# Gate of five experts as seven block products, on one Trainium2 core

## The chip, the cores and the metric

One core of a Trainium2 chip runs one program that computes a whole block: adaptive layer norm, attention, a second adaptive layer norm and a mixture of eight experts. The metric is the time of one execution in device microseconds. Lower is better.

## The reference, cut to what matters

All arrays are float32. x is 8 x 256 x 256 (batch, sequence, width), so 2048 tokens of width 256. The last part is this, with T = tokens, D = 256, E = 8 experts, F = 256, R = 64 and NL = 2 experts with low-rank terms:

```python
weights = _router_weights(x, Wr, temperature)
gate = jnp.einsum('btd,edf->ebtf', x, Wg)
up = jnp.einsum('btd,edf->ebtf', x, Wu)
gate = gate.at[:NL].add(jnp.einsum('btd,edr,erf->ebtf', x, Ga, Gb))
up = up.at[:NL].add(jnp.einsum('btd,edr,erf->ebtf', x, Ua, Ub))
mid = jax.nn.silu(gate) * up
out = jnp.einsum('ebtf,efd->ebtd', mid, Wd)
out = out.at[:NL].add(jnp.einsum('ebtf,efr,erd->ebtd', mid[:NL], Da, Db))
return jnp.einsum('bte,ebtd->btd', weights, out)
```

## The kernel before

Matrix products are made of three: an operand is split into a rounded part ("hi", type FP32R) and the remainder ("lo"), and `three` (lines 537 to 542) issues hi x hi, hi x lo and lo x hi into one place in PSUM. Each matmul has a weight load of 128 x 128.

Attention runs over 64 slots (batch b, pair of heads), slots 0 to 65 with the pipeline's ends. From slot 59 on, the first expert tiles are woven in. A tile is one expert and 512 tokens (n = 0 to 3); there are 32, in the order of `TILES`: experts 0 and 1 for n = 0 to 2, then (0, 3) and (1, 3), then experts 2 to 7 with four tiles each. In the kernel's numbering (`ORDER`) the experts with low-rank terms are 2 and 3. Tiles 0 to 3 lie in the slots; from tile 4 (`NEXT`) on a loop of its own runs on each engine (TensorE L839, ScalarE L1132, VectorE L1546, GpSimd L1724). FIRST_OF[2] is tile 8 and FIRST_OF[7] is tile 28.

In each tile m TensorE issues `up(2m)` and `up(2m+1)` (for each half of F, gate then up, 12 matmuls of 512 columns in all for each half), then `down(2m-2)` and `down(2m-1)` of the tile before (12 matmuls of 256 columns each). `ps_s` holds gate and up of one half, `ps_proj` those of the other. ScalarE makes the silu of the gate from PSUM (`gate_of`), VectorE multiplies with up (`product`), ScalarE rounds the result (`mid_head`), VectorE makes the remainder (`mid_tail`), and after the down matmuls VectorE adds the weighted result to `acc` (`accumulate`). For tiles 4 to 7 the router of the last tokens lies between these on VectorE (`LATE_ROUTE`) and ScalarE.

The weights of an expert are loaded to `raw_e`, two buffers that alternate by expert; `split_e` rounds a third of them on ScalarE and makes the remainder on GpSimd (L1660). These splits stand at the tiles of `EXPERT_STEPS`, all three of an expert at one tile, two tiles ahead of its first. The low-rank factors (64 rows) are multiplied in FP32 by `low_rank` (L756 to L766), two matmuls of 256 columns for each of six products (each is recorded as two instructions), and VectorE's `fold` adds the result to `raw_e` ahead of the split. `h2_tail` of the last batch is VectorE's remainder of the normalised tokens; tile 6 waits for it.

Every engine works through its own list in order, and all order between engines is by semaphores written out by hand. Near the end GpSimd works out the rest of the output (`rest_of_output`, `last_part`), which uses `part` of expert 7.

## Time and profile before

| | us |
|---|---|
| median of 3 runs | 808.46 |
| lowest, highest | 808.2, 809.51 |
| the profiled execution | 808.01 |
| its span | 806.3 |
| busy: TensorE | 795.3 |
| busy: VectorE | 507.5 |
| busy: ScalarE | 462.2 |
| busy: GpSimd | 395.0 |

The span is the time from the first to the last recorded instruction. In the profile PE is TensorE, PEld its weight loads, DVE VectorE, ACT ScalarE, POOL GpSimd, SP SyncE. Matmuls overlap their neighbours: what one costs is the distance between two starts, not its length.

### The profile page before, as it was taken

What the parts mean: (1) busy time and instruction counts of PE and PEld (TensorE: products, weight loads), DVE (VectorE), ACT (ScalarE), POOL (GpSimd) and SP (SyncE); (2) the same over time, 40 slices, a digit from 0 to 9 for tenths busy, and PEclk for the clock granted to TensorE, in tenths of its full rate; (3) what the DMA queues carried; (4) which work ended last, traced back from release to release, by engine and by line L of the source; (5) the groups of instructions that cost most, each with busy time, mean ns of one, the idle gap of its engine ahead of it and who ended that gap; (6) DMA issues with size and microseconds to landing.
All of it is one profiled execution on the core that took longest, in us unless ns stands there. A gap on an engine that the chain in (4) does not pass through costs nothing.

```text
span 806.3 us, 14755 instructions
## 1 busy us (share of the span) xinstructions
PE 795.3 (99%) x5116; PEld 710.1 (88%) x5116; DVE 507.5 (63%) x1074; ACT 462.2 (57%) x1255; POOL 395.0 (49%) x543
## 2 busy tenths in 40 slices
PE   9899999999999999999999999999999999999997
PEld 8688898999999999999999999899888888888887
DVE  5677676476476566557557658667785454454575
ACT  5777686677577677667767776643343232332322
POOL 3777587486576667567567656120011010110493
PEclk9999999999999999999999999999999999999999
DMA  9200010000000000000000000203010110100002
GB/s 333 103 28 2 1 61 1 1 8 2 0 8 2 1 7 2 2 2 6 1 1 8 1 2 2 79 1 94 38 40 2 40 40 1 40 0 1 1 1 105
DMA packets 8170, 21.53 MB, mean 27 GB/s; under 512 B 1561, under 2 KB 4249, under 8 KB 7969
## 3 DMA queue, kind: packets, MB, share of 16 engines
q1 hardware_dynamic: 7520, 20.51, 7.5%
q8 instruction: 42, 0.69, 0.4%
q14 instruction: 32, 0.25, 0.1%
q10 hardware_dynamic: 576, 0.08, 0.1%
HBM read 18.48 MB, written 2.11 MB: 26 GB/s over the span
## 4 chain that ended last, share of the span: by engine, by line
PE 93%; DVE 2%; POOL 1%; ACT 1%; issue 1%; DMA 1%; ACTq 0%; DVEq 0%; POOLq 0%
PE ps_o L663 14%; PE ps_proj L540 9%; PE ps_proj L542 9%; PE ps_proj L541 9%; PE ps_s L540 7%; PE ps_s L541 7%; PE ps_s L542 7%; PE ps_turn L592 4%; PE ps_y L540 4%; PE ps_y L541 4%; PE ps_y L542 4%; PE ps_turn L610 3%; PE ps_turn L540 2%; PE ps_turn L541 2%; PE ps_turn L542 2%; PE ps_o L542 2%
## 5 line engine op out<-in xcount | busy, mean ns | idle before, releaser
L663 PE MATMUL ps_o<-vaug,probs 128*128 128x129 f32 x1024 | 135.3, 275 | 1.6 <-POOL probs L1654 0.9
L663 PEld LDWEIGHTS ps_o<-vaug,probs 128*128 128x128 f32 x1024 | 129.1, 191 | 8.0 <-POOL probs L1654 1.4
L984 ACT ACTIVATE ps_s<-ps_s,knorm 128x512 f32<-128x512 f32 x128 | 79.1, 657 | 95.7 <-PE ps_s L542 95.5
L1267 DVE RECIPROCAL rden<-ps_o 128x2 f32<-128x2 f32 x128 | 21.8, 170 | 154.0 <-PE ps_o L663 153.9
L1660 POOL TENSOR_TENSOR we_lo<-raw_e,we_hi 128x512 fp32r<-128x512 f32 x22 | 28.4, 1316 | 182.3 <-ACT we_hi L1027 182.3
L1237 DVE TENSOR_TENSOR prod<-ps_proj,cs 128x1024 f32<-128x1024 f32 x76 | 92.5, 1217 | 10.9 <-ACT sq L927 10.9
L1605 POOL TENSOR_TENSOR root<-ssq,powers 128x4 f32<-128x4 f32 x76 | 77.7, 1023 | 27.6 <-ACT sq L927 27.6
L927 ACT ACTIVATE sq<-ps_proj 128x128 f32<-128x128 f32 x304 | 79.9, 278 | 18.2 <-PE ps_proj L542 15.2
L1621 POOL TENSOR_TENSOR prod<-prod 128x512 f32<-128x512 f32 x62 | 80.0, 1290 | 9.9 <-DVE prod L1237 9.9
L540 PE MATMUL ps_proj<-w_hi,h_hi 128*128 128x512 f32 x192 | 83.1, 433 | 0.9 <-DVE w_lo L1180 0.5
L1652 POOL TENSOR_SCALAR_AFFINE_SELECT probs<-probs 128x256 f32<-128x256 f32 x64 | 26.3, 410 | 106.1 <-ACT probs L992 105.8
L540 PE MATMUL ps_y<-wo_hi,oT_hi 128*128 128x256 f32 x256 | 75.8, 296 | 0.0
L542 PE MATMUL ps_proj<-w_hi,h_lo 128*128 128x512 f32 x192 | 75.7, 394 | 0.0
L541 PE MATMUL ps_proj<-w_lo,h_hi 128*128 128x512 f32 x192 | 75.4, 393 | 0.0
L1628 POOL TENSOR_TENSOR rows<-prod,rnorm 128x512 f32<-128x512 f32 x62 | 66.7, 1075 | 13.2 <-issue 4.7
L542 PE MATMUL ps_y<-wo_hi,oT_lo 128*128 128x256 f32 x256 | 71.4, 279 | 0.0
L541 PE MATMUL ps_y<-wo_lo,oT_hi 128*128 128x256 f32 x256 | 71.4, 279 | 0.0
L1044 ACT ACTIVATE mid_hi<-mid 128x512 fp32r<-128x512 f32 x64 | 40.2, 629 | 47.9 <-DVE mid L1352 26.0
L992 ACT ACTIVATE probs<-ps_s 128x1024 f32<-128x1024 f32 x64 | 66.2, 1035 | 0.0
L927 ACT ACTIVATION_READ_ACCUMULATOR sq<-ps_proj 128x1 f32 x304 | 63.4, 209 | 0.0
L1271 DVE TENSOR_TENSOR o_rows<-ps_o,rden 128x256 f32<-128x256 f32 x128 | 54.3, 424 | 4.4
L540 PE MATMUL ps_proj<-h_hi,we_hi 128*128 128x512 f32 x140 | 55.6, 397 | 0.0
(212 smaller groups left out, 2178.1 us busy)
## 6 DMA issues: line engine op xcount, KB each, us to landing
raw_e<-in_we SPq DMA_DIRECT2D x8, 768.0 KB, 4.3
raw_p<-in_wqkv SPq DMA_DIRECT2D x6, 512.0 KB, 8.1
raw_e<-in_wo SPq DMA_DIRECT2D x4, 512.0 KB, 11.6
x_all<-in_x SPq DMA_DIRECT2D x1, 1536.0 KB, 7.0
out<-acc SPq DMA_DIRECT2D x3, 512.0 KB, 2.6
x_all<-in_wmod SPq DMA_DIRECT2D x1, 1024.0 KB, 10.0
gates_a<-gate_rows_dram SPq DMA_DIRECT2D x8, 128.0 KB, 2.9
gates_b<-gate_rows_dram SPq DMA_DIRECT2D x1, 1024.0 KB, 8.0
```

The costliest lines, as they stand in the source:

```text
L540: pe.matmul(dst, hi, w_h, start=first, stop=False, skip_group_check=True)
L541: pe.matmul(dst, hi, w_l, start=False, stop=False, skip_group_check=True)
L542: return pe.matmul(dst, lo, w_h, start=False, stop=last, skip_group_check=True)
L663: mm = pe.matmul(ps_o[:, h * (D + 1):(h + 1) * (D + 1)], probs[:, s % 2, at:at + P], vaug[b % 2][:, k, i // 2, :], start=(h == 0 and k == ...
L927: squared = act.activation(sq[:, n % 2, h, :], ps_proj[:, u % 2, h * D:(h + 1) * D], ACT.Square, accum_out=ssq[:, n % 2, h:h + 1])
L984: act.activation(ps_s[:, t, :], ps_s[:, t, :], ACT.Tanh, scale=knorm[:, b % 2, t, i // 2:i // 2 + 1]).then_inc(tanh_done, 1)
L992: act.activation(probs[:, s % 2, :], ps_s[:].rearrange("p k n -> p (k n)"), ACT.Exp, scale=CAP).then_inc(exp_done, 1)
L1237: dve.tensor_tensor(prod[:, n % 2], src, cs[:, t].unsqueeze(2).broadcast_to([P, 2, 4, D]), ALU.mult).then_inc(rotated, 1)
L1271: dve.tensor_tensor(o_rows[:, t], o[:, :, 0:D], rden[:, t, :].unsqueeze(2).broadcast_to([P, 2, D]), ALU.mult).then_inc(o_rows_ready, 1)
L1605: pool.tensor_tensor(root[:, n % 2, :], ssq[:, n % 2, :], powers[:, 0:4], ALU.pow).then_inc(root_ready, 1)
L1621: pool.tensor_tensor(whole, whole, turned, ALU.add).then_inc(rot_sum, 1)
L1628: pool.tensor_tensor(rows[:, n % RING], prod[:, n % 2, 0], rnorm[:, n % 2, :].unsqueeze(2).broadcast_to([P, 4, D]), ALU.mult).then_inc(row ...
```

## The change

For the tiles 8 to 27 (experts 2 to 6) the gate is no longer made of 12 matmuls of 512 columns. The gate's weights (256 x 256) are taken as 2 x 2 blocks A of 128 x 128 and the tokens (256 x 512) as 2 x 2 blocks B of 128 x 256, and the result comes from seven block products, 21 matmuls of 256 columns, of blocks and of sums of blocks (S1 to S4 of A, T1 to T4 of B). Four products come first in the tile (`seven_first`), ScalarE copies them to SBUF (`copy_seven`), GpSimd adds pairs of them (`sums_seven`), then come the up matmuls, one down half, the last three products on top of what is in PSUM (`seven_last`) and the other down half. VectorE adds to two quarters (`add_quarters`); ScalarE makes the silu of one quarter from PSUM and of the other three at once, in place (`silu_seven`). Up always uses `ps_s`, the products `ps_proj`.

The sums need work of their own: `sums_t` (GpSimd, four operations of 128 x 256 for each n, for n = 0 and 1 in slots 63 and 64), `round_t` and `rest_t` (two operations of 128 x 512 each on ScalarE and GpSimd), `sums_s` (GpSimd, four of 128 x 128 for each expert), `round_s` and `rest_s` (128 x 512). The splits of an expert are spread, one side task in each tile. For n = 2 the tokens are written to DRAM from ScalarE's queue in slots 59 and 60 and read back.

The low-rank factors are loaded twice, to partitions 0 to 63 and 64 to 127; in A the lower half holds the rounded part and the upper the remainder, and B is rounded and its remainder made (`low_round`, `low_rest`). One product is then four matmuls of 256 columns in FP32R with 128 rows instead of two in FP32 with 64. They stand at tiles 5 (one), 6 (two), 7 (one) and 8 (two), before at 5 (two), 6, 8 and 9 (two). `part` gets a buffer for each n.

```diff
...
-LOW_STEPS = {NEXT + 1: [0, 1], NEXT + 2: [2], NEXT + 4: [3], NEXT + 5: [4, 5]}
+LOW_STEPS = {NEXT + 1: [0], NEXT + 2: [1, 2], NEXT + 3: [3], NEXT + 4: [4, 5]}
...
+SEVEN, EIGHT = FIRST_OF[NL], FIRST_OF[NE - 1]
+SEVEN_SPLIT = {FIRST_OF[e - 1] + at: (e, m3) for e in range(NL + 1, NE) for m3, at in enumerate((0, 1, 3))}
+SEVEN_SUMS = {FIRST_OF[e - 1] + 1: e for e in range(NL + 1, NE - 1)}
+SEVEN_ROUND = {FIRST_OF[e - 1] + 2: e for e in range(NL + 1, NE - 1)}
...
-                if (was := last_with(up_pair, g)) is not None:
+                if m == EIGHT:
+                    pe.wait_ge(mid_done, 2 * EIGHT)
+                elif (was := last_with(up_pair, g)) is not None:
...
+            def seven_first(m):
+                e, n = TILES[m]
+                q = m - SEVEN
+                of = blocks(m)
+                if m == FIRST_OF[e]:
...
+                    pe.wait_ge(t_split, 2 * n + 2)
+                if q:
+                    pe.wait_ge(quarter_silu, 2 * q - 1)
+                else:
+                    pe.wait_ge(mid_done, 2 * SEVEN)
+                product_of(ps_proj[:, 0, 0:S], of["A11"], of["B11"], True)
+                product_of(ps_proj[:, 0, S:], of["S2"], of["T2"], False).then_inc(seven_ready, 1)
+                if q:
+                    pe.wait_ge(quarters_added, q)
+                product_of(ps_proj[:, 1, 0:S], of["S1"], of["T1"], True)
...
+            def seven_last(m):
+                q = m - SEVEN
...
+                pe.wait_ge(seven_copied, 2 * q + 1)
+                product_of(ps_proj[:, 0, 0:S], of["A12"], of["B21"], False).then_inc(gu_ready, 1)
+                pe.wait_ge(seven_copied, 2 * q + 2)
+                product_of(ps_proj[:, 1, 0:S], of["S4"], of["B22"], False)
+                product_of(ps_proj[:, 1, S:], of["A22"], of["-T4"], False).then_inc(gu_ready, 1)
...
+                for f in range(2):
+                    pe.wait_ge(mid_done, 2 * SEVEN if m == SEVEN else 2 * m - 1 + f)
+                    for k in range(KT):
+                        mm = three(ps_s[:, f, :], we_hi[e % 2][:, 2 + k, f * P:(f + 1) * P], we_lo[e % 2][:, 2 + k, f * P:(f + 1) * P],
...
                 for k in range(KT):
...
+                    pe.matmul(dst, lowA_both[:, e, m3, at], lowB_hi[:, e, m3, :], start=(k == 0), stop=False, skip_group_check=True)
+                    mm = pe.matmul(dst, lowA_both[:, e, m3, at], lowB_lo[:, e, m3, :], start=False, stop=True, skip_group_check=True)
                 mm.then_inc(low_ready, 1)
...
+            for m in range(SEVEN, EIGHT):
+                seven_first(m)
+                up_alone(m)
+                down(2 * m - 2)
+                seven_last(m)
+                down(2 * m - 1)
+                for i in LOW_STEPS.get(m, ()):
+                    low_rank(i)
...
+            def round_t(n):
+                act.wait_ge(t_made, 4 * n + 4)
...
+                for b in range(2):
+                    act.activation(t_hi[n][:, b], h2s[n][b][:], ACT.Copy).then_inc(t_hi_done, 1)
...
+            def copy_seven(m):
+                q = m - SEVEN
...
+                    act.wait_ge(quarters_added, q)
+                for bank in range(2):
+                    act.wait_ge(seven_ready, 2 * q + bank + 1)
+                    act.activation(seven[:, 2 * bank:2 * bank + 2, :].rearrange("p a n -> p (a n)"), ps_proj[:, bank, :], ACT.Copy).then_inc(seven_copied, 1)
+            def silu_seven(m):
...
+                act.wait_ge(gu_ready, 4 * m + 3)
+                act.activation(silu[:, 0, 0:S], ps_proj[:, 0, 0:S], ACT.Silu).then_inc(quarter_silu, 1)
+                act.wait_ge(last_quarter, q + 1)
+                act.wait_ge(quarters_added, q + 1)
+                others = silu[:].rearrange("p f n -> p (f n)")[:, S:]
+                act.activation(others, others, ACT.Silu).then_inc(quarter_silu, 1)
...
+                act.activation(lowA_both[:, e], lowA[:, e], ACT.Copy).then_inc(low_rounded, 1)
+                act.activation(lowB_hi[:, e], lowB[:, e], ACT.Copy).then_inc(low_rounded, 1)
...
-                for e, m3 in EXPERT_STEPS.get(m, ()):
-                    split_e(e, m3)
+                    low_round(0)
+                    round_t(0)
+                if m == NEXT + 1:
+                    low_round(1)
+                if m == NEXT + 2:
+                    split_e(NL, 0)
+                    round_t(1)
+                if m == NEXT + 3:
+                    round_s(NL)
+                    split_e(NL, 1)
+                    split_e(NL, 2)
+                    round_t(2)
+            for m in range(SEVEN, EIGHT):
+                copy_seven(m)
+                if m in SEVEN_SPLIT:
+                    split_e(*SEVEN_SPLIT[m])
+                if m in SEVEN_ROUND:
+                    round_s(SEVEN_ROUND[m])
+                if m == SEVEN + 1:
+                    round_t(3)
+                silu_seven(m)
+                mid_head(2 * m)
...
+            def add_quarters(m):
...
+                dve.wait_ge(gu_ready, 4 * m + 4)
...
+                dve.tensor_tensor(silu[:].rearrange("p f (a n) -> p (f a) n", a=2)[:, 1:3, :], ps_proj[:, 1, :].rearrange("p (a n) -> p a n", a=2),
+                                  seven[:, 0:1, :].broadcast_to([P, 2, S]), ALU.add).then_inc(quarters_added, 1)
+            def product_seven(g):
...
+                dve.tensor_tensor(mid[:, f, :], ps_s[:, f, :], silu[:, f, :], ALU.mult).then_inc(mid_done, 1)
...
-                    dve.wait_ge(final_add, 2 * n + half - 1)
...
+            for m in range(SEVEN, EIGHT):
+                accumulate(2 * m - 2)
+                add_quarters(m)
+                for g in (2 * m, 2 * m + 1):
+                    product_seven(g)
+                for g in (2 * m, 2 * m + 1):
+                    mid_tail(g)
+                accumulate(2 * m - 1)
+                for i in LOW_STEPS.get(m, ()):
+                    fold(i)
...
+            def sums_t(n):
...
+                pool.tensor_tensor(b21, b21, b22, ALU.subtract).then_inc(t_made, 1)
...
+            def low_rest(e):
...
+                pool.tensor_tensor(lowA_both[R:P, e], lowA[R:P, e], lowA_both[R:P, e], ALU.subtract).then_inc(low_split, 1)
...
+                pool.tensor_tensor(lowB_lo[:, e], lowB[:, e], lowB_hi[:, e], ALU.subtract).then_inc(low_split, 1)
...
+            def rest_t(n):
...
+                    pool.wait_ge(t_hi_done, 2 * n + b + 1)
+                    pool.tensor_tensor(t_lo[n][:, b], h2s[n][b][:], t_hi[n][:, b], ALU.subtract).then_inc(t_split, 1)
+            def sums_s(e):
...
+                pool.wait_ge(we_split, 3 * e - 1)
+                pool.tensor_tensor(a22, a21, a22, ALU.add).then_inc(s_made, 1)
...
+                pool.tensor_tensor(a12, a12, a11, ALU.subtract).then_inc(s_made, 1)
+            def rest_s(e):
+                pool.wait_ge(s_hi_done, e - NL + 1)
+                pool.tensor_tensor(s_lo[e % 2][:], raw_e[:, e % 2, 0:KT, :], s_hi[e % 2][:], ALU.subtract).then_inc(s_split, 1)
+            def sums_seven(m):
...
+                pool.wait_ge(seven_copied, 2 * q + 1)
+                pool.tensor_tensor(seven[:, 0, :], seven[:, 0, :], seven[:, 1, :], ALU.add).then_inc(u_made, 1)
+                pool.wait_ge(seven_copied, 2 * q + 2)
+                pool.tensor_tensor(seven[:, 2, :], seven[:, 2, :], seven[:, 3, :], ALU.add).then_inc(pair_made, 1)
...
+                pool.wait_ge(mid_done, 2 * m)
+                pool.tensor_tensor(silu[:, 1, S:], seven[:, 0, :], seven[:, 2, :], ALU.add).then_inc(last_quarter, 1)
...
-            for m in range(NEXT, len(TILES)):
-                for e, m3 in EXPERT_STEPS.get(m, ()):
-                    split_e(e, m3)
+            low_rest(0)
+            rest_t(0)
+            low_rest(1)
+            split_e(NL, 0)
+            sums_s(NL)
+            rest_t(1)
+            sums_t(2)
+            rest_s(NL)
+            split_e(NL, 1)
+            split_e(NL, 2)
+            rest_t(2)
+            for m in range(SEVEN, EIGHT):
+                sums_seven(m)
+                if m in SEVEN_SUMS:
+                    sums_s(SEVEN_SUMS[m])
+                if m in SEVEN_SPLIT:
+                    split_e(*SEVEN_SPLIT[m])
+                if m in SEVEN_ROUND:
+                    rest_s(SEVEN_ROUND[m])
+                if m == SEVEN:
+                    sums_t(3)
+                if m == SEVEN + 2:
+                    rest_t(3)
             for n in range(LATE):
...
```

## Rows read from the trace of the kernel before

**Rows 1.** The profile's page: busy us, share and instructions; granted clock in 40 slices; chain.

```profile
PE 795.3 (99%) x5116; PEld 710.1 (88%) x5116; DVE 507.5 (63%) x1074; ACT 462.2 (57%) x1255; POOL 395.0 (49%) x543
...
PEclk9999999999999999999999999999999999999999
...
PE 93%; DVE 2%; POOL 1%; ACT 1%; issue 1%; DMA 1%; ACTq 0%; DVEq 0%; POOLq 0%
```

**Rows 2.** Stretches: us, busy PE PEld DVE ACT POOL, clock, DMA share, GB/s.

```profile
30.00:40.00 10.00, 7.95 (x45) 5.49 (x44) 5.26 (x10) 7.79 (x25) 9.52 (x14) 1.00 0.52 188
706.57:714.93 8.36, 8.36 (x50) 7.38 (x49) 4.34 (x9) 2.35 (x4) 0.00 (x0) 1.00 0.00 0
740.08:748.52 8.44, 8.44 (x51) 7.34 (x49) 4.31 (x9) 2.35 (x4) 0.00 (x0) 1.00 0.01 2
765.40:773.68 8.28, 8.28 (x50) 7.34 (x49) 5.69 (x9) 2.35 (x4) 8.04 (x7) 1.00 0.01 2
```

**Rows 3.** TensorE in order of time: start, length, line, operation, out<-in.

```profile
593.93 0.39 PE L540 MATMUL ps_s<-h_hi,we_hi 128*128 128x512 f32 x1
...
706.57 0.40 PE L540 MATMUL ps_s<-h_hi,we_hi 128*128 128x512 f32 x1
...
712.06 0.28 PE L540 MATMUL ps_turn<-we_hi,mid_hi 128*128 128x256 f32 x1
...
740.08 0.39 PE L540 MATMUL ps_s<-h_hi,we_hi 128*128 128x512 f32 x1
...
745.67 0.28 PE L540 MATMUL ps_turn<-we_hi,mid_hi 128*128 128x256 f32 x1
...
748.52 0.39 PE L540 MATMUL ps_s<-h_hi,we_hi 128*128 128x512 f32 x1
...
765.40 0.40 PE L540 MATMUL ps_s<-h_hi,we_hi 128*128 128x512 f32 x1
```

**Rows 4.** TensorE in order of time, at the low-rank products of tiles 5 and 6.

```profile
573.85 1.13 PE L765 MATMUL ps_y<-lowB,lowA 64*128 64x256 f32 x4
...
575.77 0.50 PE L540 MATMUL ps_s<-h_hi,we_hi 128*128 128x512 f32 x1
...
584.42 1.13 PE L765 MATMUL ps_y<-lowB,lowA 64*128 64x256 f32 x4
585.48 0.50 PE L540 MATMUL ps_s<-h_hi,we_hi 128*128 128x512 f32 x1
```

**Rows 5.** All engines in order of time, in tile 20.

```profile
700.78 0.39 PE L542 MATMUL ps_s<-h_hi,we_lo 128*128 128x512 f32 x1
...
701.21 0.69 DVE L1352 TENSOR_TENSOR mid<-ps_s,silu 128x512 f32<-128x512 f32 x1 [1.85 <-PE ps_s L542]
...
703.93 0.69 DVE L1352 TENSOR_TENSOR mid<-ps_proj,silu 128x512 f32<-128x512 f32 x1 [2.03 <-PE ps_proj L542]
...
704.54 1.48 DVE L1361 TENSOR_TENSOR mid_lo<-mid,mid_hi 128x512 fp32r<-128x512 f32 x2
...
704.66 0.63 ACT L1044 ACTIVATE mid_hi<-mid 128x512 fp32r<-128x512 f32 x1 [0.97 <-DVE mid L1352]
...
```

**Rows 6.** Groups by line and shape: busy us, mean ns of one, idle us before them.

```profile
L992 ACT ACTIVATE probs<-ps_s 128x1024 f32<-128x1024 f32 x64 | 66.2, 1035 | 0.0
...
L1037 ACT ACTIVATE silu<-ps_s 128x512 f32<-128x512 f32 x25 | 14.9, 598 | 62.8 <-PE ps_s L542 62.8
...
L1660 POOL TENSOR_TENSOR we_lo<-raw_e,we_hi 128x512 fp32r<-128x512 f32 x22 | 28.4, 1316 | 182.3 <-ACT we_hi L1027 182.3
...
L1735 POOL TENSOR_TENSOR acc<-acc,part_last 128x256 f32<-128x256 f32 x2 | 1.6, 827 | 0.0
```

**Rows 7.** VectorE in order of time, in tile 5.

```profile
573.82 0.68 DVE L1323 TENSOR_TENSOR h_lo<-h2f,h_hi 128x512 fp32r<-128x512 f32 x1
```

**Rows 8.** ScalarE in order of time, at the end of tile 7.

```profile
593.29 0.63 ACT L1044 ACTIVATE mid_hi<-mid 128x512 fp32r<-128x512 f32 x1 [1.34 <-DVE mid L1352]
```

**Rows 9.** VectorE in order of time, in tile 29.

```profile
779.98 3.50 DVE L1361 TENSOR_TENSOR mid_lo<-mid,mid_hi 128x512 fp32r<-128x512 f32 x2
```

More of the change, by code:

```diff
@@ new lines, in build @@
+        t_at = (qT_at + 2 * BLOCK, wo_at + 6 * BLOCK, h2f_at, wo_at)
+        t_hi = [place(f"t_hi{n}", [P, 2, KT, S], F32R, offset) for n, offset in enumerate(t_at)]
+        t_lo = [place(f"t_lo{n}", [P, 2, KT, S], F32R, offset + BLOCK) for n, offset in enumerate(t_at)]
+        s_hi = [place(f"s_hi{n}", [P, KT, F], F32R, wo_at + (3 - n) * BLOCK) for n in range(2)]
+        s_lo = [place(f"s_lo{n}", [P, KT, F], F32R, wo_at + (3 - n) * BLOCK + BLOCK // 2) for n in range(2)]
+        seven = place("seven", [P, 4, S], F32, probs_at + 7 * BLOCK // 2)
@@ L350, in build @@
+        h2_dram = nc.dram_tensor("h2_dram", (P, 2, KT, S), F32, kind="Internal").ap()
+        part = [place(f"part{n}", [P, 2, TT, E], F32, probs_at + BLOCK // 2 + n * BLOCK) for n in range(LATE)]
         raw_o = raw_e[:].rearrange("p a m f -> p (a m f)").rearrange("p (r k n) -> p r k n", r=RAW_RING, k=KT)
@@ L515, in _ @@
             sp.wait_ge(router, 2 * STEPS)
+            for kept in h2_kept:
+                sp.wait_ge(kept, 16)
             expert(1)
@@ L520, in _ @@
             sp.wait_ge(y_ready, B)
-            sp.dma_start(lowA[:], a["lowA"]).then_inc(low_in, 16)
-            sp.dma_start(lowB[:], a["lowB"]).then_inc(low_in, 16)
+            for half in (slice(0, R), slice(R, P)):
+                sp.dma_start(lowA[half], a["lowA"]).then_inc(low_in, 16)
+                sp.dma_start(lowB[half], a["lowB"]).then_inc(low_in, 16)
+            sp.dma_start(h2_back[:], h2_dram).then_inc(h2_back_in, 16)
             sp.dma_start(gates_b[:], gates_dram[:, E:2 * E].unsqueeze(0).broadcast_to([P, B, E])).then_inc(gates_b_in, 16)
@@ L837, in _ @@
                 slot(s)
-            for m in range(NEXT, len(TILES)):
+            for m in range(NEXT, SEVEN):
                 up(2 * m)
@@ L849, in _ @@
                     low_rank(i)
+            for m in range(SEVEN, EIGHT):
[6 more added lines that the diff above has]
+                    low_rank(i)
+            for m in range(EIGHT, len(TILES)):
+                up(2 * m)
+                up(2 * m + 1)
+                down(2 * m - 2)
+                down(2 * m - 1)
             down(2 * len(TILES) - 2)
@@ L1131, in _ @@
                 slot(s)
-            for m in range(NEXT, len(TILES)):
+            for m in range(NEXT, SEVEN):
                 gate_of(2 * m)
@@ L1144, in _ @@
                     modulate2(B - 1)
-                for e, m3 in EXPERT_STEPS.get(m, ()):
-                    split_e(e, m3)
+                    low_round(0)
[20 more added lines that the diff above has]
+                mid_head(2 * m)
+                mid_head(2 * m + 1)
+            for m in range(EIGHT, len(TILES)):
+                gate_of(2 * m)
+                gate_of(2 * m + 1)
+                mid_head(2 * m)
+                mid_head(2 * m + 1)
         @block.vector
@@ L1371, in accumulate @@
                     dve.wait_ge(base_done, 2 * n + half + 1)
-                if e == NE - 1 and 2 <= 2 * n + half < 2 * LATE:
-                    dve.wait_ge(final_add, 2 * n + half - 1)
+                if e == NE - 1 and n == 0 and half == 0:
+                    dve.wait_ge(low_ready, 3 * NL)
                 for t in range(2):
@@ L1545, in _ @@
             aggregate(B - 1)
-            for m in range(NEXT, len(TILES)):
+            for m in range(NEXT, SEVEN):
                 product(2 * m)
@@ L1565, in _ @@
                         route(LATE, piece)
+            for m in range(SEVEN, EIGHT):
[8 more added lines that the diff above has]
+                    fold(i)
+            for m in range(EIGHT, len(TILES)):
+                product(2 * m)
+                product(2 * m + 1)
+                mid_tail(2 * m)
+                mid_tail(2 * m + 1)
+                accumulate(2 * m - 2)
+                accumulate(2 * m - 1)
             accumulate(2 * len(TILES) - 2)
@@ L1669, in last_part @@
                     pool.wait_ge(base_done, 2 * n + half + 1)
-                    pool.tensor_tensor(acc[n][:, sl, :], acc[n][:, sl, :], part[:, half], ALU.add).then_inc(final_add, 1)
+                    pool.tensor_tensor(acc[n][:, sl, :], acc[n][:, sl, :], part[n][:, half], ALU.add).then_inc(final_add, 1)
             def rest_of_output(n):
@@ L1707, in slot @@
                         split_e(e, m3)
+                if s in SLOT_SUMS:
+                    sums_t(SLOT_SUMS[s])
                 return units[1:]
```

138 lines of the change are left out of this document (125 added, 13 removed).

## The prediction, made before the change was run

> **What bounds the kernel now.** The view by engine and the chain that ended last come first [rows 1]: TensorE is busy for 795.3 of 806.3 us and carries 93% of the chain, at a granted clock that is full in every slice (the 2.4 GHz level). Then the stretches of single tiles [rows 2]: in a whole tile of the expert stage TensorE is busy for all of its 8.44 or 8.36 us, VectorE for some 4.3, ScalarE for 2.35, and GpSimd for nothing in most tiles. So time is gained only by what leaves TensorE's queue, and the other engines have room for added work as long as no tile waits for it. The third view is TensorE's own order of time [rows 3]: tile 8 starts at 593.93, tile 28 at 765.40, and the 20 tiles between are the ones changed.
>
> **Part 1, the gate's matmuls.** From 740.08 to 745.67 stand the 24 matmuls of 512 columns (gate and up) of tile 25: 5.59 us, 0.233 us each; in tile 21, of an odd expert, 706.57 to 712.06, 5.49 us, 0.229 us each [rows 3]. The 24 down matmuls of 256 columns run from 745.67 to 748.52: 2.85 us, 0.119 us each. Every one of them has a weight load of its own beside it. The 12 gate matmuls thus cost 2.80 us in the 12 tiles of experts 2, 4, 6 and 2.74 us in the 8 tiles of experts 3 and 5: 33.6 + 21.9 = 55.5 us. Seven products of three matmuls of 256 columns are 21 x 0.119 = 2.50 us, in 20 tiles 50.0 us. Gain 5.5 us. The price of 0.119 is that of a down matmul, which has the same form; the ends are half of a 512 matmul (0.1145, gain 7.4 us) and 0.121 (gain 4.7 us), should the new places of the operands cost as much as the old ones differ, 2%.
> A rule on this: the Trainium skill, page "TensorE: Matmul & The Clock Gate", section "Back-to-back issue gap", gives a lone matmul at full clock N/2.4 + 2.5 ns, so 215.8 ns for 512 and 109.2 ns for 256 columns. By it the gain would be 20 x (12 x 0.2158 - 21 x 0.1092) = 5.9 us. The rows show 229 to 233 and 119 ns, so its fixed part is too small here; the 131 ns that it gives for a stream at 512 columns no row bears out.
>
> **Part 2, the low-rank products.** Eight of the FP32 instructions with 64 rows last from 573.85 to 575.77, 1.92 us; four alone from 584.42 to 585.48, 1.06 us [rows 4]. There are two such pairs and two such singles: 5.96 us. They become 24 matmuls in FP32R of 256 columns, 24 x 0.119 = 2.86 us. Gain 3.1 us (ends 2.9 and 3.6, since the first 512 matmul behind an FP32 one stands longer, 0.50 us instead of 0.39). What leaves TensorE: 5.5 + 3.1 = 8.6 us. The dropped waits on `final_add` for `part`, the two DMAs issued from ScalarE's queue at slots 59 and 60 and the read-back of `h2_back` I cost at nothing: ScalarE's waits and the slots of attention cover them; up to 0.3 us either way.
>
> **Part 3, a tile in the new order.** On TensorE: first four products 12 x 0.119 = 1.43, up 12 x 0.233 = 2.80 (ends at 4.23), down 1.43 (5.66), last three products 9 x 0.119 = 1.07 (6.73), down 1.43: 8.16 us against 8.44. The turn-around goes by measured hand-overs [rows 5]: a matmul issued at 700.78 for 0.39 releases VectorE at 701.21, VectorE's product from 703.93 for 0.69 releases ScalarE at 704.66; 0.04 us each. The last matmul of `seven_last` goes out at 6.61 and lasts 0.28 [rows 3]; `add_quarters` runs from 6.93 to 7.62; the Silu over 768 columns is not in the trace and lies between 0.598 (512) and 1.035 (1024) [rows 6], I take 0.82, to 8.48; the first product is there at 9.21, the second at 9.82; rounding 0.63 more and the two remainders end at about 11.2. TensorE asks for the first product at 8.16 + 1.43 = 9.59 (0.38 to spare), the second 1.4 later (1.2 to spare), and the remainders at 8.16 + 4.23 = 12.39 (1.2 to spare). ScalarE has 2.35 us of old work [rows 2] and gets two copies and some more Silu, about 4.4 of 8.16; GpSimd three sums of 256 columns at 0.827 and one side task of 1.3 [rows 6], 3.8 us, about 5.6 where four sums of 128 columns come with a split. All this is hidden; in a steady tile I cost it at nothing.
>
> **Part 4, the places where TensorE waits.** (a) Tile 6: the remainder of h2 of batch 7 ends at 573.82 + 0.68 = 574.50 on VectorE [rows 7], until now under the low-rank pair. With one product instead of two before it TensorE arrives at 573.85 + 0.48 = 574.33. A wait of 0.2, up to 1.0 if VectorE meets GpSimd's new `rest_t(0)`; I take 0.5.
> (b) Tile 8 waits for the remainder of S of expert 2. In ScalarE's queue `round_s` stands behind the rounding that starts at 593.29 now [rows 8]; in TensorE's queue 1.92 + 1.06 us of products become 4 x 0.48, so that it arrives at 593.93 - 1.1 = 592.8, and tile 7 starts about 1.5 earlier. The rounding thus starts between 591.8 and 593.3; then 0.63 for itself, 0.62 for `round_s`, 1.3 on GpSimd [rows 6], 0.1 of hand-overs: 594.5 to 595.9. A wait of 1.7 to 3.1, and up to 1 more because GpSimd has `sums_t(2)` and `rest_t(1)` before it and VectorE's router steps beside it. I take 2.5.
> (c) Tile 9 or so, where `sums_t(3)` lies beside the remainders of tile 8: 0 to 0.5, I take 0.2.
> (d) Tile 11 waits for `rest_t(3)`. In tile 10 the copies start when both roundings are done, at 2.4; GpSimd's three sums end at 5.6, `rest_s(3)` at 6.9, two pieces of `rest_t(3)` at 9.5, against 8.16. A wait of 0.8 to 1.9; I take 1.2.
> (e) Tile 28 goes back to the old order and its first gate matmul waits for both products of tile 27: 9.82 + 0.04 - 8.16 = 1.7 us, certain if part 3 holds.
> Sum 6.1 us (ends 4.3 and 9.3, with 0.1 either way on (e)). Between 30 and 40 us the engine is idle for 2.05 of 10 us and the clock stays granted at 1.00 [rows 2], so such a wait costs its own length and no clock.
>
> **Sum.** 8.6 gained, 6.1 waited: 2.5 us faster. The profiled execution took 808.01 us, its span 806.3 plus 1.7 around it; the median of the runs before is 808.46. That gives 805.5 for the profiled execution and 806.0 for the median; with the longer 512 matmul behind FP32 gone in four places (0.1 each) I say 805.6.
>
> **Rivals.** First, the preparations are ready in time, because ScalarE and GpSimd run ahead of their order in the tiles 4 to 7; only (e) is left: 808.46 - 8.6 + 1.7 = 801.6 us. For it speaks that GpSimd is empty there now; against it that `round_s` stands behind tile 7's last rounding by program order. Second, the slower side: VectorE and GpSimd hold each other up. A pair of remainders takes 1.48 us with GpSimd idle [rows 5] and 3.50 us beside GpSimd's stream at the end [rows 9]: 2.0 longer, 0.8 more than the 1.2 to spare. In the new order GpSimd's sums start right behind the roundings, where the second remainder runs. If that hits half of the 20 tiles, 8 us come on top: 814 us. It decides from 0.14 us a tile above what is spare on. Against it speaks that the sums can't start before the copies at 2.4, when the first remainder is over.
> The Trainium skill, page "SBUF — State Buffer", section "SBUF: two separate sides", says that of a VectorE operation with two SBUF inputs and a GpSimd operation the later one is blocked until the other is over; by that rule, which the 3.50 us agree with, the remainders wait and the products and `add_quarters`, with one operand in PSUM, do not.
> Third, the 256-column matmuls are paced by their weight loads in the new order of places; a load is shown for 0.19 us, 21 x 0.19 = 3.99 a tile, 832 us. The down matmuls at 0.119 with a load each speak against it. Fourth, the waits eat just what is saved, 808.
>
> **Numbers.** Forecast 0.66, first rival 0.12, slower one 0.15, third 0.02, fourth 0.05. The forecast's own range is 802.9 to 809.2: 808.46 - 8.6 + 4.3 less 1.3 for the far prices of parts 1 and 2, and 808.46 - 8.6 + 9.3. With most of the first rival the range is 801.0 to 809.2. About 0.2%, 1.6 us, can be told from no change. Faster than 806.8: five sixths of the forecast and the first rival, 0.67; within 0.2%: 0.14; slower: 0.19.
>
> **What would show it.** TensorE at about 2.5 us for 21 gate matmuls and 0.48 for four low-rank ones; idle time or a gap at tile 8 with GpSimd's `s_lo` as releaser (2 to 3 us), at tile 11 with `t_lo` (about 1 us), at tile 28 with VectorE's `mid` (1.7 us); none in the tiles 13 to 27. Wrong it would be if the tiles from 13 to 27 come at more than 8.2 us, or if VectorE's `mid_lo` pairs there are well over 1.5 us.

## The result: slower, 813.6 us instead of 808.5

The changed kernel took 813.58 us in the median of 9 runs (809.72 to 815.95), the kernel before 808.46 (808.02 to 809.64, 9 runs); ratio 1.0052, 95% interval 1.0033 to 1.0071. It is slower by 0.5%, outside the range. The profiled execution took 812.59 us, its span 810.9.

Three rows from the page of the changed kernel, beside [rows 1]: TensorE's busy share in 40 equal slices (in tenths), the granted clock in the same slices (9 is 90% or more), and the shares of the chain that ended last:

```profile
PE   9899999999999999999999999999879999999997
...
PEclk9999999999999999999999999999999999999999
...
PE 21%; DVE 1%; POOL 1%; issue 0%; ACT 0%; DVEq 0%; ACTq 0%
```

TensorE is busy for 789.9 us, 5.4 less than before, and still the span is 4.6 longer. Slices 29 and 30 (568 to 608 us) hold the new idle time, and the granted clock of the whole execution is 0.995. The shares of the chain add up to 23%: it is followed back only to about 625 us, GpSimd's work for tile 11, so it says nothing of the tiles 5 to 8. A look at stretches shows what a slice is too coarse for. Columns as in [rows 2]; the first five are tiles 6 and 8, the last goes from tile 25's up matmuls to tile 26's, one steady tile:

```profile
573.92:577.32 3.40, 0.64 (x6) 0.44 (x4) 3.40 (x4) 0.88 (x2) 2.96 (x3) 0.93 0.00 0
577.32:581.53 4.21, 4.21 (x12) 3.37 (x13) 2.51 (x8) 0.72 (x2) 1.64 (x1) 0.65 0.00 0
596.47:600.70 4.23, 0.64 (x7) 0.46 (x5) 4.01 (x7) 2.60 (x5) 1.96 (x3) 1.00 0.01 2
600.70:603.39 2.69, 2.69 (x13) 2.69 (x13) 2.55 (x5) 1.23 (x3) 2.69 (x3) 0.50 0.02 6
603.39:608.14 4.75, 3.30 (x13) 2.38 (x13) 4.44 (x9) 0.60 (x1) 4.26 (x5) 0.92 0.51 166
745.19:753.27 8.08, 8.08 (x60) 7.55 (x58) 4.89 (x10) 3.91 (x8) 3.46 (x4) 1.00 0.01 2
```

In the steady tile everything is as forecast: 8.08 us (said 8.16) against 8.44 and 8.36 before, TensorE never idle. The loss lies in tiles 6 and 8: TensorE works 0.64 us of 3.40 and again of 4.23, each time goes on at the 1.2 GHz level (clock 0.50 in the fourth row), and then stands once more (3.30 of 4.75). TensorE's waits in the tiles 6 to 28, in order of time; they answer to the stretches of [rows 3, 4]:

```profile
577.32 0.79 PE L596 MATMUL ps_s<-h_hi,we_hi 128*128 128x512 f32 x1 [2.76 <-DVE h_lo L1536]
...
600.70 0.54 PE L596 MATMUL ps_proj<-h_hi,we_hi 128*128 128x256 f32 x1 [3.59 <-POOL s_lo L2016]
...
608.14 0.35 PE L596 MATMUL ps_turn<-we_hi,mid_hi 128*128 128x256 f32 x1 [1.45 <-DVE acc L1618]
...
630.32 0.38 PE L596 MATMUL ps_proj<-h_hi,we_hi 128*128 128x256 f32 x1 [0.86 <-POOL t_lo L1999]
...
769.93 0.47 PE L596 MATMUL ps_s<-h_hi,we_hi 128*128 128x512 f32 x1 [1.72 <-DVE mid L1566]
```

**Where the time went, from one profiled execution to the other.** From the first low-rank product (573.85 before, 573.92 now) to tile 8's first matmul: 20.08 us before, 26.78 now, 6.7 more. From there to tile 28's first matmul: 171.47 before [rows 3], 169.23 now, 2.2 less. The rest is 40.9 and 41.0. Together 4.6. By kind: gate 20 x 2.48 = 49.6 instead of 55.5 (5.9 gained), low-rank products 24 x 0.12 = 2.9 instead of 5.96 (3.1 gained); paid are tile 6's wait 2.92 and its half clock 4.21 - 2.80 = 1.41, tile 8's wait 4.23 - 0.48 = 3.75, its half clock 2.69 - 1.42 = 1.27, the stretch to `down(14)` 4.75 - 2.80 = 1.95, tile 11 1.02, tile 28 1.88: 14.2. Gained 9.0 and paid 14.2 is 5.2 us longer, 0.6 more than the measured 4.6; 0.4 of it is the long 512-column matmul behind an FP32 one, 0.11 us each, which is gone in four places.

What stands behind the waits is on VectorE. In tile 5, the two remainders and h2's last one, which answers to [rows 7], then GpSimd beside them (the last row is `low_rest(1)`):

```profile
572.58 2.48 DVE L1586 SCALAR_TENSOR_TENSOR mid_lo<-mid,mid_hi 128x512 fp32r<-128x512 f32 x2
574.98 2.29 DVE L1536 TENSOR_TENSOR h_lo<-h2f,h_hi 128x512 fp32r<-128x512 f32 x1
```
```profile
571.51 3.00 POOL L1999 TENSOR_TENSOR t_lo<-h2f,t_hi 128x512 fp32r<-128x512 f32 x2
574.88 1.84 POOL L1991 TENSOR_TENSOR lowA_both<-lowA,lowA_both 64x768 fp32r<-64x768 f32 x1 [0.37 <-ACT lowB_hi L1231]
```

The pair takes 2.48 instead of 1.47, h_lo 2.29 instead of 0.68. In tile 8 it is the last steps of the router of the last 512 tokens, a chain of tiny operations, each of which waits for the one before:

```profile
600.90 0.96 DVE L1674 TENSOR_SCALAR r_s<-r_s 128x4 f32<-128x4 f32 x1
...
602.11 0.98 DVE L1677 TENSOR_TENSOR r_s<-r_s 128x4 f32<-128x4 f32 x1
603.12 1.23 DVE L1678 TENSOR_TENSOR r_a<-r_c,r_s 128x32 f32<-128x32 f32 x1
604.39 1.21 DVE L1679 TENSOR_TENSOR r_c<-r_a,r_b 128x32 f32<-128x32 f32 x1
...
607.12 0.88 DVE L1618 TENSOR_SCALAR acc<-ps_turn,r_wf 128x256 f32<-128x256 f32 x2
```

They end in `accumulate(12)` (the last row), which empties the bank of PSUM that `down(14)` needs. From 599.32 to 605.54 GpSimd works without a gap at `s_lo`, two splits and `rest_t(2)`. The same places in the kernel before, with TensorE's first matmul of `down(14)` as the last row:

```profile
572.42 1.47 DVE L1358 SCALAR_TENSOR_TENSOR mid_lo<-mid,mid_hi 128x512 fp32r<-128x512 f32 x2
...
597.12 0.19 DVE L1450 TENSOR_TENSOR r_a<-r_c,r_s 128x32 f32<-128x32 f32 x1
597.35 0.19 DVE L1451 TENSOR_TENSOR r_c<-r_a,r_b 128x32 f32<-128x32 f32 x1
...
598.53 0.88 DVE L1390 TENSOR_SCALAR acc<-ps_turn,r_wf 128x256 f32<-128x256 f32 x2
...
599.56 0.36 PE L540 MATMUL ps_turn<-we_hi,mid_hi 128*128 128x256 f32 x1
```

Before, `down(14)` began 0.15 us after these two operations of `accumulate(12)` ended, and 0.14 us after them in the changed kernel (608.14 against 608.00). So this hand-over had no room in the kernel before either; there TensorE just arrived at the same time.

### The profile page after: what moved, and what is told of

The parts are those of the page before. It is cut to its first block and busy times, and to the rows that moved or that the text cites. A ratio compares the mean times of both kernels' runs of the same rounds, so it can differ in the third digit from the quotient of the medians.

```text
span 810.9 us, 15401 instructions
## 1 busy us (share of the span) xinstructions
PE 789.9 (97%) x5296; PEld 716.4 (88%) x5296; DVE 528.7 (65%) x1094; ACT 494.0 (61%) x1312; POOL 486.2 (60%) x656
## 5 line engine op out<-in xcount | busy, mean ns | idle before, releaser
L2022 POOL TENSOR_TENSOR seven<-seven 128x256 f32<-128x256 f32 x20 | 15.8, 788 | 73.9 <-ACT seven L1195 73.9
L596 PE MATMUL ps_s<-qT_hi,kT_hi 128*128 128x512 f32 x128 | 50.7, 396 | 2.2 <-DVE qT_lo L1475 2.1
```

Of the source, the lines that this page charges most:

```text
L596: pe.matmul(dst, hi, w_h, start=first, stop=False, skip_group_check=True)
```

## The experiments

Theory: the path through tiles 6 to 9 is VectorE's chain (h2's last remainder, router steps, `accumulate(12)`), and GpSimd's new work stretches it. Rivals: the clock, which falls in the waits; ScalarE's and GpSimd's own queue (`s_hi`, `s_lo`, splits); VectorE's new order. Eleven kernels ran. A ratio is against the kernel before on the same chip. The part ahead of the expert tiles, which no edit is meant to touch, differs between the profiled executions (the first expert matmul stands between 494.87 and 496.63 us), so stretches within a trace are compared, not clock times alone.

### The low-rank part alone, in the kernel before

The second part of the diff (the factors stacked, `low_round` on ScalarE, `low_rest` on GpSimd) without the first.

> The kernel before with the low-rank part of the change alone (factors stacked over 128 partitions, four matmuls of FP32R for two of FP32, low_round and low_rest on ScalarE and GpSimd), the products at the tiles where they stood. If part 2 of the prediction is right the time falls by 3.1 to 3.6 us, to 805 us, because GpSimd does nothing else in tiles 5 to 8. If the low-rank preparation itself is what holds up VectorE's h2 remainder at tile 6 (GpSimd's low_rest beside it), 2 to 4 us of that come back: 807 to 809 us.

Measured: 806.28 us (804.86 to 807.27, 8 runs), ratio 0.9961 (0.9948 to 0.9974). The four matmuls of one product take 0.48 us. h_lo stands at 575.48 with 0.68, since `low_rest(0)` is over by 572.9 and `low_rest(1)` begins at 576.45. By the ratio the gain is 3.2 us, by the medians (806.28 against 808.34) 2.1, less than the 3.1 expected. In the traces it is 3.3 us from the first low-rank product to the end of the span (229.2 us against 232.5), while this execution came to that product 1.6 us later. So part 2 of the prediction holds on TensorE, and only a wait of 0.23 us in tile 5 takes something back.

### The gate part alone

```diff
-                    pe.matmul(dst, lowA_both[:, e, m3, at], lowB_hi[:, e, m3, :], start=(k == 0), stop=False, skip_group_check=True)
-                    mm = pe.matmul(dst, lowA_both[:, e, m3, at], lowB_lo[:, e, m3, :], start=False, stop=True, skip_group_check=True)
+                    mm = pe.matmul(dst, lowA[0:R, e, m3, at], lowB[0:R, e, m3, :], start=(k == 0), stop=True, skip_group_check=True)
...
-                    low_round(0)
...
-                    low_round(1)
...
-            low_rest(0)
...
-            low_rest(1)
```

> The changed kernel without its second part: the low-rank products in plain float32 from factors of 64 rows, as before, without ScalarE's four roundings and GpSimd's four remainders. If the two parts' effects add: the second part alone took 2.1 us off (806.3 against 808.3), so this kernel takes 813.6 + 2.1 = 815.7 us. Theory (the loss is GpSimd's work beside VectorE's chain in tiles 5 to 8): the four remainders (1.85 us each, 566 to 579 us) are part of that work, without them h2's last remainder is less stretched, the wait of tile 6 is under 1.5 us and its half clock gone, and 3.1 us of products come back: 813.5 to 815.

Measured: 810.72 us (809.42 to 811.87, 10 runs), ratio 1.0020 (1.0010 to 1.0029). The effects don't add, by more than the theory's own figure: alone the second part takes 0.39% off, beside the first one it puts 0.32% on (1.0020 to 1.0052). VectorE in tile 5 and TensorE's waits in tiles 6 to 8:

```profile
573.30 1.47 DVE L1581 SCALAR_TENSOR_TENSOR mid_lo<-mid,mid_hi 128x512 fp32r<-128x512 f32 x2
574.69 0.68 DVE L1531 TENSOR_TENSOR h_lo<-h2f,h_hi 128x512 fp32r<-128x512 f32 x1
```
```profile
598.14 0.36 PE L595 MATMUL ps_proj<-h_hi,we_hi 128*128 128x256 f32 x1 [2.13 <-issue]
...
605.59 0.36 PE L595 MATMUL ps_turn<-we_hi,mid_hi 128*128 128x256 f32 x1 [1.47 <-DVE acc L1613]
```

Without `low_rest(0)` in front, `rest_t(0)` runs from 567.21 to 569.73 and is over before the remainders: tile 6 has neither wait nor half clock. The wait at `down(14)` stays, and behind tile 8's wait of 2.13 us the granted clock is 0.59 for the next 2.50 us. I had expected the three microseconds of products to weigh more than the wait; the wait with what follows from it was worth more.

### Does the half clock cost the time? TensorE kept at work in the waits

```diff
+            def fill(count):
...
+                for _ in range(count):
+                    pe.matmul(ps_s[:, 1, 0:P], ident[:], ident[:], start=True, stop=True, skip_group_check=True)
...
+                if m == SEVEN:
+                    pe.wait_ge(mid_done, 2 * SEVEN - 1)
+                    fill(14)
...
+                if m == NEXT + 2:
+                    pe.wait_ge(mid_done, 2 * m - 1)
+                    fill(10)
```

> The changed kernel with 10 matmuls of the identity (128 columns) ahead of tile 6's wait and 14 ahead of tile 8's wait, on a PSUM bank that is free. The waits themselves stay. If the half clock behind the two waits (granted 0.50 from 577 to 580 and from 601 to 604) costs what the trace shows, 1.4 and 2.0 us, the time falls by about 3.4 us to 810.2 and the granted clock stays 1.00. If the waits alone are the cost, it stays at 813.6. The filling matmuls are shorter than the waits and cost nothing by either.

Measured: 813.61 us (812.6 to 813.69, 4 runs), ratio 1.0053 (1.0032 to 1.0074): nothing gained. The stretches of tiles 6 and 8, columns as above, the last one behind the start of `down(14)`:

```profile
577.32:581.53 4.21, 4.21 (x19) 3.40 (x19) 3.51 (x9) 0.83 (x2) 1.39 (x1) 1.00 0.00 0
600.70:603.39 2.69, 2.69 (x13) 1.99 (x11) 2.62 (x3) 0.68 (x2) 2.69 (x3) 1.00 0.35 64
603.39:606.60 3.21, 0.19 (x2) 0.04 (x1) 2.94 (x8) 0.00 (x0) 2.71 (x4) 1.00 0.48 191
606.60:609.00 2.40, 2.40 (x13) 2.40 (x14) 1.22 (x3) 0.63 (x1) 0.43 (x1) 0.58 0.00 0
```

The clock is full where it had been halved, and TensorE is done earlier, only to stand for 3.02 us before `down(14)`. A marker from here on is the first low-rank product behind tile 8: 612.14 us in the changed kernel, 612.11 here. Counted from the first low-rank product of tile 5, which differs a little between executions, it lies at 38.22 us in the changed kernel and at 38.45 here.

That the time is the same does not mean that the clock costs nothing. What the fill saves in tile 8 is hidden: VectorE's chain ends no sooner for it. What it saves in tile 6 is not: VectorE's chain in tile 7 begins earlier, and `down(14)` begins 32.93 us after the first product instead of 34.22, 1.3 us sooner. But the third wait, which has no fill, is now 3.02 us instead of 1.45, and the matmuls behind it run at the half clock (the last row): from `down(14)` to the marker it takes 5.52 us instead of 4.00. The edit moved a stretch of half clock and did not remove it. A kernel with all three waits filled was not run, so this run doesn't settle what the clock costs.

### h2's last remainder earlier on VectorE

```diff
                 for piece in LATE_ROUTE.get(2 * m, ()):
                     route(LATE, piece)
+                if m == NEXT + 1:
+                    h2_tail(B - 1)
                 product(2 * m + 1)
                 mid_tail(2 * m)
                 mid_tail(2 * m + 1)
-                if m == NEXT + 1:
-                    h2_tail(B - 1)
```

> The changed kernel with VectorE's remainder of h2 (batch 7) ahead of the second product and the two remainders of tile 5, nothing else moved. Theory 1, GpSimd's operations block VectorE's operations with two SBUF inputs (mid_lo and h_lo in tile 5 took 2.48 and 2.29 us beside them): the wait of 3.0 us at tile 6 and the 1.4 us of half clock behind it go, 809.5 us; tile 8 stays as it is. Theory 2, ScalarE's longer list in tile 4 makes h2 late: h_hi is rounded at 569.0 to 569.6, so the wait at tile 6 would stay at 2 us or more and the time above 812.

Measured: 810.45 us (809.38 to 811.4, 10 runs), 0.95 above what was expected, ratio 1.0020 (1.0009 to 1.0031), marker 610.16, which is 35.43 us behind the first product instead of 38.22. Tile 6 has no wait and no half clock, 4.3 us at its own place. But the next wait took over 1.5 of it: tile 8 now waits 5.12 us for `s_lo` instead of 3.59, since the router steps beside GpSimd are still stretched (0.99 us for one on 128x4).

### GpSimd's sums and `rest_t(1)` in its idle gap

```diff
             low_rest(1)
+            rest_t(1)
+            sums_t(2)
             split_e(NL, 0)
             sums_s(NL)
-            rest_t(1)
-            sums_t(2)
             rest_s(NL)
```

with `round_t(1)` a tile earlier on ScalarE, too.

> The changed kernel with rest_t(1) and sums_t(2) ahead of the split of expert 2 on GpSimd (which was idle from 579 to 587), and round_t(1) one tile earlier on ScalarE; so GpSimd does less beside the router steps of tile 7. Theory 1, the block between GpSimd and VectorE: the router steps run at their old speed, the waits at tile 8 (3.8 us and 1.9 us) fall to 1.6 to 2 and 0, and with them the half clock there (2 us): 808 to 809 us. Theory 2, ScalarE's list: round_s stands behind the same rounding and nothing changes, 813.

Measured: 810.53 us (807.98 to 811.63, 10 runs), ratio 1.0019 (1.0006 to 1.0033), marker 610.95 (36.28 us behind the first product). That is less than the 808 to 809 expected, and its interval only touches that of the changed kernel (1.0033 to 1.0071). Tile 7's router steps are back at 0.17 to 0.42 us. Tile 6 keeps its wait (2.92 us) and its half clock; `down(14)` waits 3.02 for `accumulate(12)`, as the steps of tile 8 are still 0.97 to 1.24 us long beside GpSimd's splits. Behind this wait the clock stays at 1.00.

### Both edits together, and with GpSimd held back

The second kernel has besides

```diff
             split_e(NL, 1)
+            pool.wait_ge(router, STEPS * (LATE + 1))
             split_e(NL, 2)
             rest_t(2)
```

> The changed kernel with both earlier edits together: the remainder of h2 earlier on VectorE, and rest_t(1), sums_t(2) in GpSimd's idle stretch. Theory (the path through tiles 6 to 9 is VectorE's chain h2 remainder, router steps of the last tokens, accumulate(12), and GpSimd's operations stretch its steps): each edit alone took off one part of it (810.45 and 810.53 against 813.6); together the wait of tile 6 is gone, router steps 0 to 7 run at their old length, and what is left is the slowed stretch of steps 8 to 12 in tile 8: low-rank product 4 starts at 607.5 to 609 us, time 807.5 to 809.5. Rival (the two edits take off the same delay, since the last event before down(14) is GpSimd's or ScalarE's own chain s_hi, s_lo, splits): no better than either, 810 to 810.5.

> As the kernel with both edits, and GpSimd starts split (2, 2) and rest_t(2) only when the router of the last tokens is done. Theory (GpSimd's operations stretch VectorE's small steps): the last steps of the router, 0.83 to 1.24 us each beside them, come back towards the 0.17 to 0.19 us that they took in the kernel before; down(14) waits under 1 us; time 805 to 807. Rival (the steps are long for another reason, for example the semaphore between them): their lengths stay, and the time is that of the kernel with both edits or longer, since GpSimd's work is only later.

Measured: both edits 808.53 us (807.83 to 809.32, 10 runs), ratio 0.9997 (0.9988 to 1.0007), marker 607.51; held back 806.43 (805.95 to 808.08, 9 runs), ratio 0.9976 (0.9966 to 0.9986), marker 605.07. VectorE's steps in the two kernels, first with both edits, then held back:

```profile
597.47 0.98 DVE L1677 TENSOR_TENSOR r_s<-r_s 128x4 f32<-128x4 f32 x1
598.48 1.24 DVE L1678 TENSOR_TENSOR r_a<-r_c,r_s 128x32 f32<-128x32 f32 x1
599.75 1.21 DVE L1679 TENSOR_TENSOR r_c<-r_a,r_b 128x32 f32<-128x32 f32 x1
```
```profile
598.28 0.16 DVE L1677 TENSOR_TENSOR r_s<-r_s 128x4 f32<-128x4 f32 x1
598.48 0.19 DVE L1678 TENSOR_TENSOR r_a<-r_c,r_s 128x32 f32<-128x32 f32 x1
598.70 0.19 DVE L1679 TENSOR_TENSOR r_c<-r_a,r_b 128x32 f32<-128x32 f32 x1
```

Three operations take 3.43 us beside GpSimd and 0.54 without it, and TensorE's wait before `down(14)` is gone. From the last low-rank product of tile 7 to the marker it is 15.53 us (from 591.98) and 12.22 (from 592.85), 3.3 less, where the medians differ by 2.1. Not all of that is GpSimd's. The stretches behind tile 8's wait (3.43 us in the first kernel, 3.38 in the second), first with both edits, then held back, up to the marker:

```profile
596.05:598.55 2.50, 2.50 (x13) 2.50 (x14) 2.36 (x5) 1.22 (x3) 2.50 (x3) 0.60 0.02 7
```
```profile
596.86:605.07 8.21, 8.21 (x58) 7.67 (x58) 6.37 (x18) 2.83 (x6) 6.34 (x6) 1.00 0.29 98
```

Behind nearly the same wait the clock is halved in one trace and full in the other. In the first the halving costs nothing, since `down(14)` waits for VectorE anyway. In the second TensorE begins `down(14)` at 601.14, 0.4 us after VectorE is done, and the 24 matmuls before it take 4.28 us instead of 5.83. With a half clock there too, 1.8 of the 3.3 us would be left (an estimate from these rows); only that much is GpSimd's for certain. GpSimd only did its work later, and the kernel is 2.1 us faster in the medians: it was never short of GpSimd's time.

### The block by itself, in the kernel before

Idle work for GpSimd in the kernel before, with no part in the result: six operations from the rounding of h2's last tokens on, eight from tile 7's gate on. The first kernel adds blocks of 128x512, which reads two and writes one; the second one only writes, 128x1536 each time, about as long for each. The line of the first kernel, then that of the second:

```diff
+                    pool.tensor_tensor(spare_a, spare_a, spare_b, ALU.add).then_inc(dummy, 1)
...
+                    pool.memset(spare_w, 0.0).then_inc(dummy, 1)
```

> The kernel before with idle work for GpSimd: six additions of two 128x512 blocks of SBUF from the time that h2 of the last tokens is rounded (tile 5), and eight from the start of tile 7's gate. They take part in no result. Theory (VectorE's operations with SBUF operands wait while GpSimd reads): the remainder h_lo of 128x512, 0.68 us in the kernel before, takes 1.4 to 2.5 us, mid_lo pairs 2.0 to 3.5 instead of 1.47, and the router's steps of tile 7 and 8, 0.17 to 0.43 us, take 0.6 to 1.3 beside the additions; TensorE waits in tile 6, time 810 to 814. Rival (the changed kernel's own new work on VectorE made them late, not GpSimd): no duration changes by more than 0.1 us, time within 0.5 us of 808.3.

> The same places with as many memsets of 128x1536 in the additions' stead, which read nothing and only write. If reading two operands is what VectorE waits for: durations on VectorE stay as in the kernel before, time within 0.7 us of 808.3. If any use of SBUF by GpSimd blocks: as with the additions, 810 us or more.

Measured: 819.94 us with the additions (2 runs), ratio 1.0137 (1.0117 to 1.0158); 808.12 with the memsets (807.95 to 809.46, 8 runs), ratio 0.9993 (0.9982 to 1.0003). VectorE in tiles 5 and 7 with the additions, and then with the memsets:

```profile
575.15 1.75 DVE L1327 TENSOR_TENSOR h_lo<-h2f,h_hi 128x512 fp32r<-128x512 f32 x1
...
595.50 1.09 DVE L1434 TENSOR_SCALAR r_s<-r_s 128x4 f32<-128x4 f32 x1
...
598.52 1.40 DVE L1442 TENSOR_TENSOR r_eq<-r_eq,tri 128x256 f32<-128x256 f32 x1
```
```profile
573.91 0.69 DVE L1327 TENSOR_TENSOR h_lo<-h2f,h_hi 128x512 fp32r<-128x512 f32 x1
...
590.02 0.17 DVE L1434 TENSOR_SCALAR r_s<-r_s 128x4 f32<-128x4 f32 x1
...
591.75 0.43 DVE L1442 TENSOR_TENSOR r_eq<-r_eq,tri 128x256 f32<-128x256 f32 x1
...
595.56 0.36 DVE L1450 TENSOR_SCALAR r_s<-r_s 128x4 f32<-128x4 f32 x1
```

GpSimd is busy beside all of these in both kernels (567.59 to 576.34 and 567.39 to 575.97 for the first row). It is the reading that stretches VectorE's two-input operations. The time of 819.94 is far above the 810 to 814 expected. TensorE's two waits in the tiles 5 to 8 of that kernel:

```profile
577.03 2.07 PE L769 MATMUL ps_turn<-lowB,lowA 64*128 64x256 f32 x4 [1.78 <-DVE r_log L1321]
...
609.24 0.55 PE L544 MATMUL ps_turn<-we_hi,mid_hi 128*128 128x256 f32 x1 [3.98 <-DVE acc L1394]
```

Both are for VectorE, the second for `accumulate(12)` behind the stretched chain, and the granted clock behind each is 0.50 (577.03 to 580.00 and 609.24 to 612.00). The splits of weights are not the cause: the memsets put off the third one as well (from 594.90 to 598.86), at no cost. The last row shows a one-input step at 0.36 instead of 0.17 beside a memset, small but there. The Trainium skill, page "SBUF — State Buffer", section "SBUF: two separate sides", says that GpSimd and VectorE take a pair of ports as an exclusive lock, an operation with two SBUF inputs only against a GpSimd operation that reads SBUF; the pair of kernels agrees, 1.75 against 0.69 us.

### The waits of tiles 11 and 28, and the s-chain

Held back as above, and besides `rest_t(3)` ahead of tile 10's sums on GpSimd, and tile 28 begins in the pair of banks that is free; the second kernel also moves ScalarE's rounding of S:

```diff
-    return 0 if g < 2 * LATE else (g + 1) % 2
+    return 0 if g < 2 * LATE else g % 2 if g >= 2 * EIGHT else (g + 1) % 2
...
                 mid_head(2 * m)
+                if m == NEXT + 3:
+                    round_s(NL)
                 mid_head(2 * m + 1)
...
                 if m == NEXT + 3:
-                    round_s(NL)
```

> The changed kernel with both earlier edits, GpSimd held until the router is done, and two more: rest_t(3) goes ahead of tile 10's sums on GpSimd (wait of 1.1 us in tile 11), and tile 28 starts in the pair of banks that is free (wait of 1.9 us). Theory (every wait that is left costs its own length): 806.4 - 1.1 - 1.9 = 803.4 us (802.8 to 804). Rival (the time at the end is set by something else, so that waits in late tiles are hidden): 805.5 to 806.4.

> As the kernel before it in this list, and ScalarE rounds s (2) between tile 7's two roundings of mid instead of after them, so that GpSimd's s_lo ends at about 594.9 instead of 596.8. Theory (down(14) waits for accumulate(12), which ends VectorE's router chain, not for s_lo): the first wait of tile 8 shrinks by about 1.5 to 2 us and the wait of down(14) grows by as much, since VectorE's chain is no shorter: 0 to 0.6 us gained, 802.6 to 803.6. Rival (s_lo is what tile 8 waits for): the full 2 us, 801.4.

Measured: 803.84 us (802.54 to 804.88, 4 runs), ratio 0.9929 (0.9912 to 0.9947), and 802.13 (802.06 to 802.6, 4 runs), ratio 0.9911 (0.9894 to 0.9927). The first is 2.6 us below the kernel held back in the medians (3.8 by the ratios), near the 3.0 of the two waits; from the marker to the end of the span it is 196.3 us instead of 199.1, 2.8 less. The second leads by 1.7 in the medians, with intervals that overlap, where I had said at most 0.6. But in the traces, which differ by 1.2, 0.7 of it stands before the edit: the last low-rank product of tile 7 is at 593.01 in the first and at 592.28 in the second. From there to the marker it is 12.27 and 11.73 us, so 0.54 belongs to the edit, as the theory had it. TensorE's waits in tile 8 of the second kernel:

```profile
594.45 0.36 PE L596 MATMUL ps_proj<-h_hi,we_hi 128*128 128x256 f32 x1 [1.54 <-POOL s_lo L2021]
...
596.70 0.50 PE L596 MATMUL ps_s<-h_hi,we_hi 128*128 128x512 f32 x1 [0.59 <-POOL we_lo L1910]
...
600.01 0.36 PE L596 MATMUL ps_turn<-we_hi,mid_hi 128*128 128x256 f32 x1 [0.26 <-DVE acc L1622]
```

Three small waits are left where 3.4 us stood, the last of them for `accumulate(12)`. This kernel beats the one before and the changed one.

## Why the prediction was wrong

**Parts 1 and 3 held.** 21 gate matmuls took 2.48 us (said 2.50), a steady tile 8.06 to 8.13 (said 8.16), with no wait in the tiles 12 to 27; the Silu over 768 columns took 0.85 (said 0.82).

**Part 2 held on TensorE and failed beside the rest.** The gain of 3.1 us is there (0.48 for four matmuls), and with nothing else changed it arrives in the trace (3.3 from the first product on), if not in full in the median (2.1). What the sum left out is the second part's work on GpSimd, four remainders of 1.84 to 2.16 us, which pushed `rest_t(0)` onto h2's last remainder. Only "up to 1.0 if VectorE meets GpSimd's new `rest_t(0)`" stood in (a).

**Part 4 is the step that failed:** "Sum 6.1 us (ends 4.3 and 9.3...)" was 14.2. Point by point: (a) "I take 0.5" was 2.9 of wait and 1.4 of half clock. (b) "I take 2.5" was 3.75 of wait, which is inside its range of 1.7 to 4.1, but 1.27 of half clock and 1.95 up to `down(14)` stand behind it; that wait for `accumulate(12)` is not in the list at all, although `down(14)` began right behind it in the kernel before (0.15 us): VectorE's chain had no room there. (c) none, said 0.2. (d) 1.0, said 1.2. (e) 1.9, said 1.7. In (b) I had followed the queue of ScalarE and GpSimd, and gave VectorE's router steps a share in "up to 1 more", as if they were safe because they are short. They are 27 steps that each wait for the last one, so most of them (the reductions and reciprocals kept their length) can be held up by a whole GpSimd operation of 1.3 us.

**The claim on the clock was wrong; what that cost stays open.** "Such a wait costs its own length and no clock" came from a stretch with many short pauses [rows 2]. Here one pause of 2.9 and one of 3.75 us were each followed by matmuls at the 1.2 GHz level. Of the 14.2 us, 2.7 are that half clock, and about 0.3 more stand in the stretch up to `down(14)`. Filling the two pauses changed nothing in the time, but a new stretch at the half clock stood behind the third and cost 1.5 us. Over the nine executions of the changed kernel the time goes with the clock: 813.58 to 815.95 us where the mean granted clock is 0.991 to 0.993, 809.72 to 812.59 where it is 0.995 to 0.997. The profiled one, at 0.995, is of the second kind, so the trace shows less of the loss than the median has.

**The second rival had the mechanism and nearly the time (814), in the wrong place.** It looked at mid_lo pairs of the 20 steady tiles and asked for 0.14 us beyond what is spare; there the pairs meet nothing (1.29 us for two). The same block fell on the tiles 5 to 8, before the steady order begins, where the new work for it is prepared. Its 0.15 should have been more: [rows 9] had shown 3.50 instead of 1.48, and all the preparations of parts 1 and 2 were new reading on GpSimd beside a VectorE that was busy for 21.63 of 27 us there (573 to 600 us in the kernel before). GpSimd was busy for 3.83 us of that stretch before and is for 15.35 now. The trace of the kernel before even shows one router step that met a split:

```profile
594.90 1.30 POOL L1660 TENSOR_TENSOR we_lo<-raw_e,we_hi 128x512 fp32r<-128x512 f32 x1 [7.96 <-ACT we_hi L1027]
...
595.01 1.23 DVE L1443 SCALAR_TENSOR_TENSOR r_c<-r_a,r_fb 128x32 f32<-128x32 f32 x1
```

Beside memsets the same step takes 0.19 us.

What stays open: in which share the 4.6 us divide between h2's remainder, the router steps and the half clock that follows from the waits. The edits overlap (each took 0.3% off, both 0.55%, and holding GpSimd back 0.2% more), so no single number belongs to either.

## What to carry to other kernels

An engine that idles is not free to be used if its work stretches that of a busy one. Before work is moved onto GpSimd, list what VectorE runs in the same microseconds, and price each two-input operation there at up to its own length plus one whole GpSimd operation, above all in a chain of short dependent steps; if the work can wait, let it wait for the end of that chain. The steady state of a new order may be right and the loss lie in the few tiles that lead into it, so these are worth a timeline of their own.
